# A two-layer token kernel: who masks the first energies of the second attention's later steps, when GpSimd masks the others, and where the gelu table is loaded

## The chip, the cores and the metric

The kernel runs on one core of one Trainium2 chip. The metric is device time in microseconds (us) of one execution. The engines are called TensorE (PE), VectorE (DVE), ScalarE (ACT), GpSimd (POOL) and SyncE (SP) here; PE's weight loads are a lane of their own (PEld) in the profile.

## What is computed

Input: 8192 tokens (32 x 256) of 128 features, all fp32. Two layers, each of the form x = x + attention(norm(x)) + mixture_of_experts(norm(x)). Layer 0 has a linear attention and a gated expert layer with a shared expert. Layer 1, in which the change lies, is:

```python
q = elu(x @ Wq.T + bq); k = elu(x @ Wk.T + bk)          # 8 heads of 16
v = silu(x @ Wv.T + bv); u = silu(x @ Wu.T + bu)
mask = tril(ones(256, 256))
energy = einsum('bhnd,bhmd->bhnm', q, k) * mask          # no softmax
out = einsum('bhnm,bhmd->bhnd', energy, v)
x_att = (u * rms_norm(out, scale)) @ Wo.T + bo

probs = softmax(x @ w_router.T); top 2 of 8 experts per token
h = gelu(x @ w1[e] + b1[e])                              # 128 -> 512
out = sum over the two experts of gate * (h @ w2[e] + b2[e])
```

Only the blocks of 128 x 128 on the diagonal of the mask need a mask; the off-diagonal half comes from a running state.

## The kernel before, in words

The tokens are 16 groups of 512 (`NG` = 16). The program is written out by hand for each engine; each engine runs its list in order, and semaphores tie them together. Its parts in time are the first attention with the shared expert (to about 150 us), the 36 expert tiles of layer 0 (to about 410 us), the second attention (to about 640 us), and the 36 expert tiles of layer 1 to the end.

**The second attention** is a software pipeline of steps 2 to 17. In step s, group g = s - 2 gets its q, k, v and u, group e = s - 3 its energies and their product with v, and groups y = s - 4 and x = s - 5 their norm and their addition to x. A group's energies come in two sets, i = 2e and i = 2e + 1. Each set fills two pairs of PSUM banks of 128 x 1024: `pair[2]` and `pair[3]`.

- PE computes a set (L1101). `energies(e, 1)` may overwrite the banks only when both halves of `energies(e, 0)` are read.
- DVE multiplies `pair[2]` by the causal mask on the way to SBUF (L1718, `mask_energies`).
- ACT copies `pair[3]` to SBUF unmasked (L2095, `copy_energies`), and POOL masks that copy in place (L2321, `affine_select`). For the last two groups (e >= `DVE_MASKS` = 14) DVE masks the copy in place (L1724).
- PE multiplies the masked sets by v (`gather`, L1124).

**What else DVE does in a step.** In order: q's elu (L1690), adding a finished group to x (L1743), `mask_energies(e, 0)`, k's elu (L1690), routing arithmetic and `shift` (L1282), v (L1699), `mask_energies(e, 1)`, u (L1706), the state (L1710), and `gated` (L1731). In steps 3, 4 and 6 to 10 it also joins layer 0's expert results to x (`collect0`, L1655), eight instructions of 128x128 with both inputs in SBUF. Step 10 does the last join (group 15). Routing arithmetic (L1288 to L1408) is small instructions of 128x128 or less, most with both inputs in SBUF.

**What POOL does in a step.** Eight indirect transfers, numbered 0 to 7 (gathers of expert results, L2215, or sends of routed rows, L2204); between them two masks, and a power for the root (L2326, or L2331 `powers`, which DVE's next L1736 waits for). Each of the first transfers waits for a semaphore of PE's step (`behind_attention1`). The order before is: transfers 0, 1, mask of set 2e, 2, 3, mask of set 2e + 1, root, 4, 5, 6, `powers`, 7.

Of the kernel before, what the change touches and what calls it, by code (L numbers as in the profile page):

```python
# [12 lines left out]
ACT = mybir.ActivationFunctionType  # L13
AX = mybir.AxisListType.X

P = 128
# [4 lines left out]
NG = NT // GT  # L21
# [88 lines left out]
LEAD = 2  # L110
# [2 lines left out]
STEPS0 = NG + LEAD + 2  # L113
STEPS1 = NG + LEAD + 3
DVE_MASKS = NG - 2


NSTAGE, NIN, NOUT, NJOIN, NGATE, AHEAD = (8, 4), 4, 4, 3, 2, 6
# [41 lines left out]
def with_root(y):  # L160

    return STATS[1].get(y + LEAD + 2, (None,))[0]
# [7 lines left out]
def masked_by_dve(e):  # L170

    return e >= DVE_MASKS


def columns_before(layer, step):
# [77 lines left out]
def build(nc, t, out):  # L253
    const_np, at = constants()
    with ExitStack() as ctx:
        pe, dve, act, pool, sp = nc.tensor, nc.vector, nc.scalar, nc.gpsimd, nc.sync
# [74 lines left out]
        def const(name):  # L331
            a, n = at[name]
            return consts[:, a:a + n]

        ident = const("ident")
# [172 lines left out]
        def blocks(ap, b=P):  # L508
            return ap.rearrange("p (a b) -> p a b", b=b)
# [165 lines left out]
        def tensor_program():  # L675
# [409 lines left out]
            def energies(e, s):  # L1085

                i = 2 * e + s
                if i == 0:
                    pe.wait_ge(ranks_read, NS + 1)
                    pe.wait_ge(out_ready, NTILES)  # L1090
                    pe.wait_ge(hid_ready, 2 * NTILES)
                if i >= 1:
                    pe.wait_ge(en_dve, i)
                    pe.wait_ge(en_copied, i)
                pe.wait_ge(q1_ready, e + 1)
                pe.wait_ge(kh1_ready, e + 1)
                for tile in range(GT):
                    tok = slice(tile * P, (tile + 1) * P)
                    for r in range(ROWTILES):
                        part = slice(32 * r, 32 * r + 32)  # L1100
                        m = pe.matmul(bank[4 + r][:, tok], kh1[e % 2][s][part, tok], q1[e % 2][part, tok], start=True, stop=True)  # L1101
                m.then_inc(en_done, 1)
# [14 lines left out]
            def gather(e, s):  # L1117
                i = 2 * e + s
                pe.wait_ge(en_dve, i + 1)
                pe.wait_ge(en_masked, i + 1)  # L1120
                for tile in range(GT):
                    for j in range(ROWTILES):
                        c = ((j % 2) * GT + tile) * P
                        m = pe.matmul(bank[3][32 * j:32 * j + 32, tile * P:(tile + 1) * P],  # L1124
                                      v_heads[e % 2][:, tile, j, s:s + 2, :].rearrange("p s d -> p (s d)"), en1[j // 2][i % 2][:, c:c + P],
                                      start=False, stop=(s == HEADS32 - 1 and tile == GT - 1), skip_group_check=True)
                m.then_inc(av_done, 1)
# [122 lines left out]
        def vector_program():  # L1250
# [462 lines left out]
            def mask_energies(e, s):  # L1713
                i = 2 * e + s
                dve.wait_ge(en_done, i + 1)
                if i >= 2:
                    dve.wait_ge(av_done, i - 1)
                dve.tensor_tensor(blocks(en1[0][i % 2][:]), blocks(pair[2][:]),  # L1718
                                  const("causal").unsqueeze(1).to_broadcast([P, 8, P]), ALU.mult).then_inc(en_dve, 1)

            def mask_copied(e, s):
                i = 2 * e + s
                dve.wait_ge(en_copied, i + 1)
                dve.tensor_tensor(blocks(en1[1][i % 2][:]), blocks(en1[1][i % 2][:]),  # L1724
                                  const("causal").unsqueeze(1).to_broadcast([P, 8, P]), ALU.mult).then_inc(en_masked, 1)

# [102 lines left out]
        def scalar_program():  # L1829
# [267 lines left out]
            def squares(e):  # L2097
                act.wait_ge(uo_ready, e + 1)
                if e >= 1:
                    act.wait_ge(ss_done, e)  # L2100
                act.activation(sq1[:], bank[3], ACT.Square).then_inc(sq_ready, 1)
# [7 lines left out]
            for step in range(LEAD, NG + LEAD):  # L2109
                g, e, y = step - LEAD, step - LEAD - 1, step - LEAD - 2  # L2110
                new, old, last = 0 <= g < NG, 0 <= e < NG, 0 <= y < NG
                if new and g >= 1:
                    minus_exp(q1_done, g, 0, e1[0], q1_max, q1_exp)
                    minus_exp(k1_done, g, 1, e1[1], k1_max, k1_exp)
                if last:
                    squares(y)
                if old:
                    copy_energies(e, 0)
                if new:
                    tanh1(v1_done, g, 0, th1[0], v1_ready, v1_tanh)  # L2120
                if has_sums(1, step):
                    keep_sums(1, step, 0 if last else P, P * (1 + len(LOGITS[1].get(step, ()))))
                if new:
                    queries1(g)
                if old:
                    copy_energies(e, 1)
                if last:
                    totals(y)
                if step in LOGITS[1]:
                    keep_logits(1, step)  # L2130
                if new:
                    tanh1(u1_done, g, 1, th1[1], u1_ready, u1_tanh)
                    if step == LEAD:
                        columns(1, EX_LATER[0], 6)
                    keys_by_token(g)
                for n in COLUMNS[1].get(step, ()):
                    if n not in EX_LATER:
                        normalise(1, n)

                two = len(COLUMNS[1].get(step, ())) > 1  # L2140
                if new and not two:
                    heads1(g)
                for k, n in enumerate(COLUMNS[1].get(step, ())):
                    columns(1, n, 1 - k)
                if new and two:
                    heads1(g)
                for _, s, names in ROUTE[1].get(step, ()):
                    if "b" in names:
                        exponentials(1, s)

            squares(NG - 2)
            copy_energies(NG - 1, 0)
            copy_energies(NG - 1, 1)
# [34 lines left out]
        def pool_program():  # L2188
# [128 lines left out]

            def mask_energies(e, s):
                i = 2 * e + s
                pool.wait_ge(en_copied, i + 1)  # L2320
                pool.affine_select(out=blocks(en1[1][i % 2][:]), in_=blocks(en1[1][i % 2][:]), pattern=[[0, 8], [1, P]], compare_op=ALU.is_ge,  # L2321
                                   fill=0.0, base=0, channel_multiplier=-1).then_inc(en_masked, 1)

# [9 lines left out]
            for step in range(LEAD, NG + LEAD + 1):  # L2333
# [12 lines left out]
                            send(1, *sends[i - len(gathers)])  # L2346

                transfer(0)
                transfer(1)
                if old and not masked_by_dve(e):  # L2350
                    mask_energies(e, 0)
                transfer(2)
                transfer(3)
                if old and not masked_by_dve(e):
                    mask_energies(e, 1)
                if last and with_root(y) is None:
                    roots(y)
                transfer(4)
# [76 lines left out]
```

## Time and profile before

| | |
|---|---|
| median of 3 runs | 897.45 us (894.57 to 899.02) |
| the profiled execution | 900.08 us, of which the span is 898.5 us |
| PE busy | 92% of the span |
| DVE busy | 78% |
| POOL busy | 69% |
| ACT busy | 65% |
| second attention, 421.0 to 627.0 us | 206 us for steps 3 to 17, 12.5 to 15 us each |

Times are from the start of the span. The profile is of one execution, so what is worked out of it is compared with 900.08 us, not with the median. Within a step of the second attention the shares differ much from those of the whole: DVE is busy for 10.8 to 14.2 us of each step.

### The profile page before, as it was taken

What the parts mean: (1) busy time and instruction counts of PE and PEld (TensorE: products, weight loads), DVE (VectorE), ACT (ScalarE), POOL (GpSimd) and SP (SyncE); (2) the same over time, 40 slices, a digit from 0 to 9 for tenths busy, and PEclk for the clock granted to TensorE, in tenths of its full rate; (3) what the DMA queues carried; (4) which work ended last, traced back from release to release, by engine and by line L of the source; (5) the groups of instructions that cost most, each with busy time, mean ns of one, the idle gap of its engine ahead of it and who ended that gap; (6) DMA issues with size and microseconds to landing.
All of it is one profiled execution on the core that took longest, in us unless ns stands there. A gap on an engine that the chain in (4) does not pass through costs nothing.

```text
span 898.5 us, 22649 instructions
## 1 busy us (share of the span) xinstructions
PE 827.5 (92%) x7937; PEld 737.8 (82%) x7937; DVE 700.3 (78%) x1812; ACT 581.1 (65%) x1190; POOL 623.8 (69%) x599
## 2 busy tenths in 40 slices
PE   5789989999899989998898889898999999999996
PEld 3678878889799989986665666566899999999995
DVE  6787788987577987897889998999765566567776
ACT  5756465545366667768887777665776666666660
POOL 4157777777005788785888888888877777777662
PEclk9999999999999989999999999999999999999998
DMA  9799998116659997972111111113766555678976
GB/s 264 236 372 357 357 353 296 53 54 192 216 165 274 319 304 225 288 226 78 42 42 37 37 41 42 44 42 121 288 186 213 176 173 186 198 236 268 290 248 206
DMA packets 130995, 173.98 MB, mean 194 GB/s; under 512 B 15810, under 2 KB 85954, under 8 KB 130628
## 3 DMA queue, kind: packets, MB, share of 16 engines
q1 hardware_dynamic: 96864, 124.43, 42.6%
q0 software_dynamic: 16640, 34.37, 11.9%
q10 hardware_dynamic: 17380, 13.73, 5.1%
q8 instruction: 65, 1.06, 0.5%
q14 instruction: 46, 0.38, 0.1%
HBM read 93.64 MB, written 80.97 MB: 194 GB/s over the span
## 4 chain that ended last, share of the span: by engine, by line
PE 48%; DVE 26%; issue 7%; POOL 6%; ACT 5%; SPq 5%; DMA 3%; DVEq 0%; ACTq 0%; POOLq 0%
PE pair L977 14%; PE pair L913 5%; PE pair L915 5%; PE pair L914 5%; POOL sent L2204 4%; PE pair L944 3%; PE pair L822 3%; DVE a_en L1718 2%; PE pair L733 2%; DVE X L1655 2%; DVE stats_t L1266 2%; SPq L618 2%; ACT a_rows L1845 2%; SPq L590 1%; PE pair L1101 1%
## 5 line engine op out<-in xcount | busy, mean ns | idle before, releaser
L2204 POOL DMA_INDIRECT sent<-a_rows,slot x224 | 224.0, 1000 | 68.1 <-issue 64.5
L2215 POOL DMA_INDIRECT ex_joined<-outs,slot x128 | 135.5, 1059 | 88.9 <-DMA outs<-ex_tile_out 50.5
L913 PE MATMUL pair<-ex_x_hi,ex_w_hi 128*128 128x256 f32 x497 | 146.5, 295 | 0.2 <-issue 0.2
L915 PE MATMUL pair<-ex_x_hi,ex_w_lo 128*128 128x256 f32 x497 | 140.4, 282 | 0.0
L914 PE MATMUL pair<-ex_x_lo,ex_w_hi 128*128 128x256 f32 x497 | 140.3, 282 | 0.0
L2306 POOL DMA_INDIRECT back<-ex_tile_out,slot x104 | 113.9, 1096 | 36.8 <-issue 26.5
L977 PE MATMUL pair<-ex_down_all,ex_hid 128*128 x1136 | 133.3, 276 | 0.5 <-issue 0.3
L977 PEld LDWEIGHTS pair<-ex_down_all,ex_hid 128*128 128x128 f32 x1136 | 129.7, 192 | 2.3 <-issue 2.3
L2019 ACT ACTIVATE ex_hid<-pair,ex_stage 128x256 f32<-128x256 f32 x284 | 107.5, 491 | 6.8 <-PE pair L915 3.4
L1881 ACT ACTIVATE ex_w_hi<-ex_stage 128x768 fp32r<-128x768 f32 (+1 forms) x72 | 67.4, 937 | 52.4 <-DMA ex_stage<-in_experts 52.4
L913 PEld LDWEIGHTS pair<-ex_x_hi,ex_w_hi 128*128 128x128 f32 x497 | 94.8, 191 | 0.6 <-issue 0.6
L914 PEld LDWEIGHTS pair<-ex_x_lo,ex_w_hi 128*128 128x128 f32 x497 | 94.7, 191 | 0.0
L915 PEld LDWEIGHTS pair<-ex_x_hi,ex_w_lo 128*128 128x128 f32 x497 | 94.6, 190 | 0.0
L1483 DVE TENSOR_TENSOR ex_w_lo<-ex_stage,ex_w_hi 128x768 fp32r<-128x768 f32 (+1 forms) x72 | 77.2, 1072 | 6.2 <-ACT ex_w_hi L1881 5.8
L944 PE MATMUL pair<-ex_stage,ex_hid 128*128 128x128 f32 x568 | 71.3, 280 | 0.9 <-DVE ex_hid L1611 0.9
L1627 DVE TENSOR_TENSOR ex_tile_out<-pair,ex_b2o 128x512 f32<-128x512 f32 (+1 forms) x31 | 20.6, 666 | 64.5 <-PE pair L977 64.5
L944 PEld LDWEIGHTS pair<-ex_stage,ex_hid 128*128 128x128 f32 x568 | 68.2, 196 | 2.1 <-issue 1.7
L2009 ACT ACTIVATE ex_gate_s<-pair 128x512 f32<-128x512 f32 (+1 forms) x72 | 42.2, 587 | 32.0 <-PE pair L915 27.3
L1489 DVE TENSOR_TENSOR ex_x_lo<-pair,ex_x_hi 128x512 fp32r<-128x512 f32 x72 | 48.9, 680 | 14.9 <-ACT ex_x_hi L1887 14.4
L1611 DVE TENSOR_TENSOR ex_hid<-ex_gate_s,pair 128x512 f32<-128x512 f32 (+1 forms) x72 | 48.9, 680 | 9.7 <-ACT ex_gate_s L2009 6.5
L1845 ACT ACTIVATE a_rows<-X,shift,rstd 128x128 f32<-128x128 f32 x88 | 36.2, 485 | 30.8 <-DVE shift L1282 30.8
L1887 ACT ACTIVATE ex_x_hi<-pair 128x512 fp32r<-128x512 f32 x72 | 42.4, 588 | 20.1 <-PE pair L733 20.0
(269 smaller groups left out, 2025.7 us busy)
## 6 DMA issues: line engine op xcount, KB each, us to landing
outs<-v_heads SPq DMA_DIRECT2D x8, 4352.0 KB, 37.7
ex_stage<-in_experts SPq DMA_DIRECT2D x72, 322.0 KB, 3.5
ex_stage<-in_experts SPq DMA_DIRECT2D x72, 320.0 KB, 5.0
ex_tile_in<-sent SPq DMA_DIRECT2D x72, 128.0 KB
outs<-ex_tile_out SPq DMA_DIRECT2D x71, 128.0 KB
ex_joined<-back ACTq DMA_DIRECT2D x15, 512.0 KB, 5.8
ex_tile_in<-sent SPq DMA_DIRECT2D x54, 132.0 KB
X<-in_x SPq DMA_DIRECT2D x16, 256.0 KB, 5.0
```

Of the source, the lines that this page charges most:

```text
L913: pe.matmul(o[:, of_half], wh, x_hi[i % 2][:, of_half], start=True, stop=False)
L914: pe.matmul(o[:, of_half], wh, x_lo[i % 2][:, of_half], start=False, stop=False)
L915: m = pe.matmul(o[:, of_half], wl, x_hi[i % 2][:, of_half], start=False, stop=True)
L944: m = pe.matmul(bank[7][:, i * C:(i + 1) * C], hid[n % 2][c][:, i * P:(i + 1) * P], stage[0][n % NSTAGE[0]][:, i // HALF, 2 * F0P + c * C: ...
L977: m = pe.matmul(bank[b][:, s * C:(s + 1) * C], hid[n % 2][c][:, s * P:(s + 1) * P], down_all[:, bass.ds(experts[s // HALF], 1), c * C:(c + ...
L1483: dve.tensor_tensor(w_lo[layer][n % NSTAGE[layer]][:, 0:k, 0:u], stage[layer][n % NSTAGE[layer]][:, 0:k, 0:u], w_hi[i % 2][:, 0:k, 0:u].bi ...
L1845: m = act.activation(r[:, (g % GPS) * GT + j, 0:C], X[:, n, :], ACT.Identity, bias=shift[:, n:n + 1], scale=inverse_of(layer, g)[:, j:j + 1])
L1881: act.activation(w_hi[i % 2][:, 0:k, 0:u], stage[layer][n % NSTAGE[layer]][:, 0:k, 0:u], ACT.Copy).then_inc(w_hi_here, 1)
L2019: m = act.activation(hid[n % 2][c][:, of_half], bank[bank_of_up1(n, c)][:, of_half], ACT.Gelu, bias=stage[1][n % NSTAGE[1]][:, h, b1:b1 + 1])
L2204: pool.indirect_dma_start(out=sent[layer], out_offset=bass.IndirectOffsetOnAxis(ap=slot_i[layer][k][:, s, j:j + 1], axis=0), in_=rows[laye ...
L2215: pool.indirect_dma_start(out=joined[g % NJOIN][:, j, k, :], out_offset=None, in_=outs, in_offset=bass.IndirectOffsetOnAxis(ap=slot_i[0][k ...
L2306: pool.indirect_dma_start(out=back, out_offset=bass.IndirectOffsetOnAxis(ap=address_of(n)[:, s // HALF, s % HALF:s % HALF + 1], axis=0), i ...
```

## The change

Three edits.

1. **First masks of late steps.** For even sets i = 2e with 8 <= e < 14 (steps 11 to 16, behind the last join) DVE masks `pair[3]` too, straight from PSUM, right behind `pair[2]`. ACT's copy and POOL's mask of these six sets are gone. `en_dve` is signalled behind the second of the two.
2. **POOL's masks.** Where POOL still masks, the mask of set 2e stands behind transfer 0 instead of 1, and that of set 2e + 1 behind transfer 2 instead of 3 (steps 3 to 16).
3. **Gelu.** Behind its last step and ahead of `squares(14)`, ACT runs a gelu of 1x8 on constants.

```diff
+FROM_PSUM = max(s for s in STATS[1] if STATS[1][s] == (NG - 1,)) - LEAD      # 8
+def masked_from_psum(i):
+    return i % 2 == 0 and FROM_PSUM <= i // 2 < DVE_MASKS
+def copies_before(i):
+    return sum(not masked_from_psum(j) for j in range(i))
...
 # tensor_program, energies(e, s)
                 if i >= 1:
                     pe.wait_ge(en_dve, i)
-                    pe.wait_ge(en_copied, i)
+                    pe.wait_ge(en_copied, copies_before(i))
...
 # tensor_program, gather(e, s)
-                pe.wait_ge(en_masked, i + 1)
+                pe.wait_ge(en_masked, copies_before(i + 1))
...
 # vector_program, mask_energies(e, s)
-                dve.tensor_tensor(blocks(en1[0][i % 2][:]), blocks(pair[2][:]),
-                                  const("causal").unsqueeze(1).to_broadcast([P, 8, P]), ALU.mult).then_inc(en_dve, 1)
+                m = dve.tensor_tensor(blocks(en1[0][i % 2][:]), blocks(pair[2][:]), const("causal").unsqueeze(1).to_broadcast([P, 8, P]), ALU.mult)
+                if masked_from_psum(i):
+                    m = dve.tensor_tensor(blocks(en1[1][i % 2][:]), blocks(pair[3][:]), const("causal").unsqueeze(1).to_broadcast([P, 8, P]), ALU.mult)
+                m.then_inc(en_dve, 1)
...
 # scalar_program, a step
-                if old:
+                if old and not masked_from_psum(2 * e):
                     copy_energies(e, 0)
...
+            act.wait_ge(q1_max, NG)
+            act.activation(e1[0][0:1, 0:8], ident[0:1, 0:8], ACT.Gelu)
             squares(NG - 2)
...
 # pool_program, a step
                 transfer(0)
+                if old and not masked_by_dve(e) and not masked_from_psum(2 * e):
+                    mask_energies(e, 0)
                 transfer(1)
-                if old and not masked_by_dve(e):
-                    mask_energies(e, 0)
                 transfer(2)
-                transfer(3)
                 if old and not masked_by_dve(e):
                     mask_energies(e, 1)
+                transfer(3)
```

POOL's queue from the end of step 9 through step 10, before. `powers` is step 9's; `sent` and `ex_joined` rows are transfers; `a_en_111` is the copy of set 2e, `a_en_112` that of set 2e + 1.

```order
L2331 TENSOR_TENSOR powers<-bases,halves_of 128x8
L2215 DMA ex_joined_144<-outs,slot 128x128
L2204 DMA sent<-ex_rows_147,slot 69632x132 x2
L2321 AFFINE_SELECT a_en_111<-a_en_111 128x1024
L2204 DMA sent<-ex_rows_147,slot 69632x132 x2
L2321 AFFINE_SELECT a_en_112<-a_en_112 128x1024
L2204 DMA sent<-ex_rows_147,slot 69632x132 x3
```

The same place in the changed kernel.

```order
L2346 TENSOR_TENSOR powers<-bases,halves_of 128x8
L2230 DMA ex_joined_144<-outs,slot 128x128
L2219 DMA sent<-ex_rows_147,slot 69632x132
L2336 AFFINE_SELECT a_en_111<-a_en_111 128x1024
L2219 DMA sent<-ex_rows_147,slot 69632x132 x2
L2336 AFFINE_SELECT a_en_112<-a_en_112 128x1024
L2219 DMA sent<-ex_rows_147,slot 69632x132 x4
```

Both masks stand one transfer sooner; the number of instructions is the same.

POOL's queue in step 11, before.

```order
L2204 DMA sent<-a_rows_85,slot 69632x132 x2
L2321 AFFINE_SELECT a_en_111<-a_en_111 128x1024
L2204 DMA sent<-a_rows_85,slot 69632x132 x2
L2321 AFFINE_SELECT a_en_112<-a_en_112 128x1024
L2326 TENSOR_TENSOR rms<-rms,halves_of 128x4
```

The same place in the changed kernel.

```order
L2219 DMA sent<-a_rows_85,slot 69632x132 x3
L2336 AFFINE_SELECT a_en_112<-a_en_112 128x1024
L2219 DMA sent<-a_rows_85,slot 69632x132
L2341 TENSOR_TENSOR rms<-rms,halves_of 128x4
```

The mask of set 2e is gone, and the other has three transfers ahead of it instead of four and a mask.

DVE's queue in step 13, before: from the addition to x to v. `a_en_109` is the masked `pair[2]` of set 2e, and the small instructions on `gatev` and `cells` are routing.

```order
L1743 SCALAR_TENSOR_TENSOR X<-pair,rms,X 128x128 x4
L1718 TENSOR_TENSOR a_en_109<-pair,consts 128x1024
L1690 SCALAR_TENSOR_TENSOR a_k<-pair,bqk1p,a_e_94 128x512
L1339 TENSOR_REDUCE gatev<-route 128x16
L1340 TENSOR_TENSOR cells<-route 128x128
L1341 TENSOR_REDUCE gatev<-cells 128x16
```

The same place in the changed kernel.

```order
L1756 SCALAR_TENSOR_TENSOR X<-pair,rms,X 128x128 x4
L1729 TENSOR_TENSOR a_en_109<-pair,consts 128x1024
L1731 TENSOR_TENSOR a_en_111<-pair,consts 128x1024
L1701 SCALAR_TENSOR_TENSOR a_k<-pair,bqk1p,a_e_94 128x512
L1350 TENSOR_REDUCE gatev<-route 128x16
L1351 TENSOR_TENSOR cells<-route 128x128
```

A second instruction of 128x1024 stands ahead of k's elu; all behind it keeps its order.

## Rows read from the trace of the kernel before

**Rows 1.** Chain that ended last, 412 to 500 us; columns: start, us, what.

```profile
by line: POOL sent L2204 20.1%; issue 11.9%; DVE X L1655 8.7%; DVE a_en L1718 5.7%; POOL a_en L2321 5.0%; POOL ex_joined L2215 4.4%; POOL powers L2331 3.9%; PE pair L1101 3.8%; DVE X L1743 3.1%; DVE a_u L1706 2.9%; POOL rstd L2198 2.4%; DVE
...
476.17 1.69 POOL powers L2331
```

**Rows 2.** Chain that ended last, 626 us to the end, by line.

```profile
by line: PE pair L977 46.7%; PE pair L913 12.6%; PE pair L915 12.4%; PE pair L914 12.4%; PE pair L733 5.7%; DMA ex_joined<-back 2.2%; PE pair L1101 1.0%; PE pair L1124 0.8%; DVE X L1666 0.8%; issue 0.8%; DVE X L1665 0.7%; DVE a_en L1718 0.5
```

**Rows 3.** DVE in order of time, steps 7 and 8: start, us, instruction, idle before.

```profile
479.35 1.22 DVE L1718 TENSOR_TENSOR a_en<-pair,consts 128x1024 f32<-128x1024 f32 x1
...
481.13 1.56 DVE L1282 SCALAR_TENSOR_TENSOR shift<-moments,powers 128x4 f32<-128x4 f32 x1
...
484.42 0.67 DVE L1706 SCALAR_TENSOR_TENSOR a_u<-a_th,pair 128x512 f32<-128x512 f32 x1
485.01 2.23 DVE L1655 SCALAR_TENSOR_TENSOR X<-ex_joined,gates_tok,X 128x128 f32<-128x128 f32 x4
...
487.49 1.25 DVE L1655 SCALAR_TENSOR_TENSOR X<-ex_joined,gates_tok,X 128x128 f32<-128x128 f32 x4
...
494.74 1.22 DVE L1718 TENSOR_TENSOR a_en<-pair,consts 128x1024 f32<-128x1024 f32 x1
...
499.31 0.69 DVE L1706 SCALAR_TENSOR_TENSOR a_u<-a_th,pair 128x512 f32<-128x512 f32 x1 [0.57 <-ACT a_th L2082]
```

**Rows 4.** Busy time of line L1655 in steps 7 to 10: us, DVE busy.

```profile
478.00:534.90 56.90, 12.52 (x32) 1.00 0.13 39
```

**Rows 5.** POOL in order of time, step 7.

```profile
485.07 1.10 POOL L2321 TENSOR_SCALAR_AFFINE_SELECT a_en<-a_en 128x1024 f32<-128x1024 f32 x1
...
490.42 1.66 POOL L2331 TENSOR_TENSOR powers<-bases,halves_of 128x8 f32<-128x8 f32 x1 [0.42 <-DVE bases L1273]
```

**Rows 6.** DVE in order of time, steps 11, 13, 15 and 16.

```profile
539.13 1.25 DVE L1289 TENSOR_TENSOR cells<-logit,gatev 128x128 f32<-128x128 f32 x1
540.42 0.32 DVE L1290 TENSOR_TENSOR cells<-cells,consts 128x128 f32<-128x128 f32 x1
...
565.50 1.54 DVE L1340 TENSOR_TENSOR cells<-route 128x128 f32<-128x128 f32 x1
...
592.68 0.99 DVE L1330 CAST slot<-gatev 128x16 int32<-128x16 f32 x1
593.71 0.17 DVE L1331 CAST slot<-gatev 128x16 int32<-128x16 f32 x1
...
596.65 0.58 DVE L1363 CAST starts_i<-ends 128x8 int32<-128x8 f32 x1
...
605.58 1.67 DVE L1388 TENSOR_TENSOR cells<-tiles_f,cells 128x136 f32<-128x136 f32 x1
```

**Rows 7.** DVE in order of time, step 13, a mask and what follows.

```profile
563.40 1.22 DVE L1718 TENSOR_TENSOR a_en<-pair,consts 128x1024 f32<-128x1024 f32 x1
564.53 0.74 DVE L1690 SCALAR_TENSOR_TENSOR a_k<-pair,bqk1p,a_e 128x512 f32<-128x512 f32 x1
```

**Rows 8.** PE in order of time, steps 11, 14 and 18.

```profile
543.72 0.66 PE L680 MATMUL pair<-consts,a_rows 128*128 128x128 f32 x4 [0.38 <-DVE a_u L1706]
...
578.46 0.22 PE L711 MATMUL pair<-choice_bf,before_bf 128*128 128x128 bf16 x1 [0.88 <-DVE choice_bf L1305]
...
579.50 1.17 PE L1101 MATMUL pair<-a_q,a_kh 32*128 32x128 f32 x32 [0.77 <-DVE a_en L1718]
...
628.58 1.70 PE L1101 MATMUL pair<-a_q,a_kh 32*128 32x128 f32 x32 [1.71 <-DVE a_en L1718]
```

**Rows 9.** Two stretches: us, busy PE, PEld, DVE, ACT, POOL, granted PE clock, DMA.

```profile
577.50:580.70 3.20, 1.55 (x40) 1.21 (x36) 3.10 (x8) 1.30 (x4) 2.70 (x4) 1.00 0.13 42
629.00:632.40 3.40, 3.40 (x52) 2.54 (x48) 3.40 (x4) 2.08 (x3) 2.79 (x3) 0.51 0.95 382
```

**Rows 10.** Start of layer 1's expert tiles, ACT and PE in order of time.

```profile
639.64 1.28 ACT L2019 ACT_TABLE_LOAD   x1
...
641.92 0.36 PE L913 MATMUL pair<-ex_x_hi,ex_w_hi 128*128 128x256 f32 x1 [0.17 <-issue]
```

More of the change, by code:

```diff
@@ L1717, in mask_energies @@
                     dve.wait_ge(av_done, i - 1)
-                dve.tensor_tensor(blocks(en1[0][i % 2][:]), blocks(pair[2][:]),
-                                  const("causal").unsqueeze(1).to_broadcast([P, 8, P]), ALU.mult).then_inc(en_dve, 1)
+                m = dve.tensor_tensor(blocks(en1[0][i % 2][:]), blocks(pair[2][:]), const("causal").unsqueeze(1).to_broadcast([P, 8, P]), ALU.mult)
+                if masked_from_psum(i):
+                    m = dve.tensor_tensor(blocks(en1[1][i % 2][:]), blocks(pair[3][:]), const("causal").unsqueeze(1).to_broadcast([P, 8, P]), ALU.mult)
+                m.then_inc(en_dve, 1)
             def mask_copied(e, s):
                 i = 2 * e + s
-                dve.wait_ge(en_copied, i + 1)
+                dve.wait_ge(en_copied, copies_before(i + 1))
                 dve.tensor_tensor(blocks(en1[1][i % 2][:]), blocks(en1[1][i % 2][:]),
@@ L2319, in mask_energies @@
                 i = 2 * e + s
-                pool.wait_ge(en_copied, i + 1)
+                pool.wait_ge(en_copied, copies_before(i + 1))
                 pool.affine_select(out=blocks(en1[1][i % 2][:]), in_=blocks(en1[1][i % 2][:]), pattern=[[0, 8], [1, P]], compare_op=ALU.is_ge,
```

## The prediction

> **What bounds the kernel now.** I read the chain that ended last first, cut at the stretches of the change. From 626 us to the end it is PE almost alone: four matmul lines hold 84% [rows 2]. The reader is to see that nothing behind the second attention can swallow or add time: whatever the second attention gains is handed on one to one. In the second attention up to 500 us the chain runs over POOL's transfers (L2204 20%, L2215 4%), POOL's masks (5%) and `powers` (4%), and over DVE [rows 1]. It still passes `powers` at 476.17, the one that DVE waits for at the start of step 7 [rows 1]. So to step 6 POOL is the bound, and its list gets no shorter there; from step 7 on DVE is, with PE a little behind it.
>
> Next I read DVE instruction by instruction, and looked for rows much longer than their own kind. They are the core of this case. The addition of a join takes 1.25 us for four (487.49), but 2.23 at 485.01 [rows 3], and POOL's mask runs from 485.07 to 486.17 [rows 5]. `shift` takes 1.56 us for 4 columns [rows 3]. In steps 11, 13, 15 and 16 one small routing instruction each takes 1.25, 1.54, 0.99 and 1.67 us, where its like takes 0.32 or 0.17 [rows 6]. Each of them lies under a mask of POOL. So POOL's mask costs DVE time when DVE meets it with an instruction whose inputs are in SBUF, and costs none under L1718, L1690 or L1706, which read PSUM.
>
> **Edit 2, masks one transfer sooner, steps 3 to 10.** Nothing is added. A mask moves ahead by about 1.3 us (a transfer of 0.97 and the 0.30 in front of it) against DVE's work. The second mask then lies under L1718 and u instead of under the joins. In steps 7 to 10 L1655 holds DVE for 12.52 us in 32 instructions [rows 4]; eight quartets of 1.25 [rows 3] would be 10.0, so 2.5 us are waits. Of the 0.98 in step 7 I leave 0.2, because everything ahead of the join also starts sooner there: gain 2.3 us. The first mask stood over `shift`. What this is worth is less than the stall itself, since u has a floor: from the mask at 494.74 to u at 499.31 are 4.57 us although DVE stood idle for 0.57 of them, waiting for PE and ACT [rows 3]. Step 7 took 5.07 (479.35 to 484.42) [rows 3]: gain 0.5. In steps 8 to 10 the floor is already met: gain 0. In steps 3 to 6 DVE loses several us to masks as well, but POOL's own list sets the time. It could run `powers` of step 6 only some 0.3 us sooner: gain 0.3, with 0 and 1.8 as ends. Behind step 7 POOL has little slack itself (0.42 idle ahead of `powers` [rows 5]), and takes back 0.2 by step 10. Sum of edit 2: -2.9 us, with ends 0 and -4.5.
>
> **Edit 1, six first masks by DVE.** Added: six instructions like L1718. One holds DVE for 1.13 us (563.40 to 564.53) [rows 7]: 6.8 us in all. Removed: six copies on ACT, which isn't waited for there, and six masks on POOL, whose worth is what DVE waits for under them [rows 6]. By steps, in us:
>
> - 13, 15, 16, where DVE itself is the chain: 1.13 - (1.54 - 0.29) = -0.1; 1.13 - (0.99 - 0.17) = +0.3; 1.13 - (1.67 - 0.30) = -0.2.
> - 11: DVE alone would lose 1.13 - 0.93 = 0.2. But PE's `energies(e, 1)` waits for `en_dve`, which comes 1.13 later, and PE's list behind it must reach L680, where it now waits 0.38 for u [rows 8]. So PE is late by 0.75: +0.7.
> - 14: PE stood 0.77 for the mask at 579.50 [rows 8], and no mask of POOL is in DVE's way: +1.1, all of it on the chain.
> - 12: PE has no wait and DVE some: between 0 and 1.13, +0.6.
>
> The set 2e + 1 is masked by POOL sooner too, as a mask and a transfer ahead of it are gone. The earliest is when ACT has copied it, and DVE is by then at v and L1718, which read PSUM. It also leaves the cast at 596.65 (0.58 instead of 0.17) [rows 6]: -0.4. Sum of edit 1: +2.4 - 0.4 = +2.0 us, with ends 0 and +6.8.
>
> One price isn't in DVE's list. PE stood 1.71 us ahead of 628.58 [rows 8], and right behind that wait the granted clock was 0.51 over 629.0 to 632.4 (the lower of the two levels, 1.2 GHz) [rows 9]. In step 14 PE stood 0.88 and 0.77 with two short matmuls between, and the clock stayed 1.00 [rows 8, 9]. The second wait now becomes 0.77 + 1.13 = 1.90, so that of some 3 us hardly 0.3 are work. That is more idleness than what was punished at 628. I take one fall there. Half clock for 3.4 us would lose at most 1.7; some of it falls on waits, so +1.3, with ends 0 and 1.7.
>
> **Edit 3, gelu's table.** The load of 1.28 us stands at 639.64 on ACT, in front of the first gelu. PE lacks only 0.17 us there (641.92), as it has matmuls of the next tile ahead [rows 10]. The new place is in a wait of ACT for u's product. Gain 0.2, ends 0 and 0.5.
>
> **Sum.** -2.9 + 2.0 + 1.3 - 0.2 = +0.2 us on the profiled 900.08, which lies 2.6 above the median of 897.45. Moved to the median: 897.6, which I round to 897.5.
>
> **A rule weighed.** DVE's L1388 began at 605.58, and undisturbed would have ended at 605.88; POOL's mask is recorded from some 0.1 us after that. It took 1.67 all the same [rows 6]. The Trainium skill (SBUF — State Buffer, Who interferes with whom) says that the pair of ports shared by DVE and GpSimd is an exclusive lock for a whole instruction, and that the order of issue decides who waits. By that order DVE should have won here and at 565.50, and the long rows would have another cause that the change leaves in place.
>
> **Rivals.**
>
> - **A cause other than the mask (0.05).** If the waits at 565.50 and 605.58 aren't the mask's, 1.25 + 1.37 = 2.6 us of edit 1's return is missing: +2.8, 900.3 us. Against it: no such row is found in steps 12 and 14, where the first mask met PSUM instructions. The lock's order of issue, named above, is what speaks for it.
> - **The masks only change their victims (0.13).** The moved masks meet other SBUF instructions, since DVE too starts sooner. Edit 2 then gives 0.5 instead of 2.9: +2.6, 900.0 us. It decides where the second mask still overlaps L1655 by 1 us in steps 8 to 10.
> - **The clock falls in each step with a lengthened wait (0.12), slower.** In steps 11, 13, 14 and 16 `energies(e, 1)` waits up to 1.13 us longer for DVE. If PE falls to 1.2 GHz in all four, three more falls at 1.3 come on top: +0.2 + 3.9 = +4.1, 901.6 us, and with the ends of edit 1 a little over 902. It decides where waits of 1.5 us suffice; at 628.58 it took 1.71 [rows 8].
> - **The joins were worth more, and the added masks are hidden (0.15), faster.** If POOL follows DVE in steps 5 and 6, 1.5 more come back, and if PE and DVE have slack in steps 11 to 16, edit 1 costs nothing and no clock falls: -2.9 - 1.5 - 0.2 = -4.6, 892.9 us. POOL's chain up to 476 speaks against the first half [rows 1], the 0.77 in step 14 against the second.
>
> **How the numbers follow.** My case, gains and losses that cancel, gets 0.55; its own range is 895 to 900.5, which holds the sum without a fall of the clock (-1.1) too. The range 892.5 to 902 reaches to the fast and the slow rival. About 0.5%, or 4.5 us, is what a measurement of this kernel can tell from no change. Only the fast rival and the tails cross it below (0.17), only the clock rival's upper half and tails above (0.10); the rest, 0.73, is no change.
>
> **What would show it.** In the changed profile: L1655 in steps 7 to 10 busy for about 10.2 us instead of 12.5. Routing instructions in steps 11, 13, 15 and 16 all near 0.3. DVE's two masks back to back, 1.13 apart, and PE waiting for the second ahead of `energies(e, 1)`, 1.9 in step 14. A granted clock under 1 in step 14. ACT's table load before 627 us. POOL idle in steps 12 to 16 where it never was. The first add of the expert phase's chain begins within 1.5 us of where it began. The prediction is wrong if DVE meets masks of POOL in places that I took as free, or if a wait for `powers` or a root appears on DVE.

## The result, and the profile after

The changed kernel took 901.33 us (median of 20 runs, 897.34 to 904.55), the kernel before 898.86 us (20 runs on the same chip, 894.57 to 900.73). The ratio is 1.0029, 95% interval 1.0015 to 1.0042: slower by some 2.6 us (1.3 to 3.8). That lies inside the forecast range of 892.5 to 902 us, and within the 0.5% that the forecast called no change. The forecast was a balance of +0.2 us. The gains and losses that it named are there, but some of their sizes are off, and the profile and the experiments show which.

The profiled execution of the changed kernel took 901.92 us, of which the span is 900.5. The first part of its page:

```profile
span 900.5 us, 22638 instructions
## 1 busy us (share of the span) xinstructions
PE 828.0 (92%) x7937; PEld 738.5 (82%) x7937; DVE 695.0 (77%) x1818; ACT 576.4 (64%) x1185; POOL 618.4 (69%) x593
```

The shares say nothing here: six instructions more on DVE, six fewer on POOL and six copies fewer on ACT. What tells is the length of each step. I take it as the time from a step's first mask on DVE (L1718 before, L1729 after) to the next step's. In the table, rows e1 to e12 are the experiments of the next section. The lengths are worked out from the rows of that line, with the granted clock of step 14 beside them, in all profiled executions on chips where the kernel before runs in 897 to 899 us:

| us | 3-6 | 7-10 | 11 | 12 | 13 | 14 | 15 | 16 | clock in 14 |
|---|---|---|---|---|---|---|---|---|---|
| before | 57.39 | 57.68 | 12.53 | 13.84 | 14.83 | 11.37 | 13.87 | 12.70 | 1.00 |
| after | 57.76 | 55.17 | 13.42 | 14.08 | 16.88 | 14.04 | 14.34 | 13.06 | 0.88 |
| e1, edit 2 | 57.81 | 55.15 | 12.29 | 13.53 | 16.03 | 14.00 | 13.38 | 11.99 | 0.76 |
| e2, edit 1 | 57.41 | 57.68 | 13.42 | 14.11 | 15.35 | 14.05 | 14.12 | 12.90 | 0.88 |
| e3, edit 3 | 57.42 | 57.72 | 12.53 | 13.85 | 14.82 | 12.91 | 14.16 | 11.97 | 0.87 |
| e4, short masks | 57.75 | 55.17 | 12.50 | 13.45 | 14.39 | 11.58 | 13.20 | 12.12 | 1.00 |
| e9, chosen steps | 57.40 | 55.18 | 12.29 | 13.50 | 14.29 | 12.90 | 13.38 | 11.97 | 0.87 |
| e10, copied | 57.42 | 57.70 | 14.13 | 13.85 | 15.26 | 13.10 | 15.37 | 13.28 | 0.87 |
| e11, copied, late | 57.41 | 57.71 | 13.77 | 14.84 | 16.10 | 14.16 | 14.76 | 15.79 | 0.88 |
| e12, split signal | 57.40 | 57.67 | 13.41 | 14.09 | 15.30 | 15.14 | 14.09 | 12.87 | 0.78 |

Steps 3 to 13 repeat to some 0.03 us where nothing touches them, and that is what makes this table worth more than ten totals. Steps 15 and 16 repeat only where step 14 had the same clock. In e3, which changes nothing in them, they took 14.16 and 11.97 us behind a slower step 14, against 13.87 and 12.70 before: POOL's masks met other instructions of DVE (1.55 us at L1326 and 0.74 at L1387, instead of 0.99 at L1330 and 1.67 at L1388). The table also sets right two ranges given for the kernel before: its steps 3 to 17 took 10.8 (step 17) to 15.4 us, and DVE was busy for only 9.5 us of step 14.

The totals aren't that steady. Step 3's first mask started anywhere from 418.0 to 423.8 us in these executions, though no code ahead of it differs. After against before, steps 3 to 16 took 4.54 us more, the changed kernel entered them 3.95 us sooner by chance, and took 1.4 more behind them: the 2.0 us between the two spans.

**Edit 2 in the profile after.** Line, engine, shape, count, busy us and mean ns, over steps 7 to 10:

```profile
L1666 DVE SCALAR_TENSOR_TENSOR X<-ex_joined,gates_tok,X 128x128 f32<-128x128 f32 x32 | 10.0, 355 | 0.3
```

10.0 us instead of 12.52 [rows 4]; no join meets a mask there any more. But DVE now waits longer for POOL's `powers` ahead of step 7 (0.61 us before) and also ahead of step 11 (no such wait before), and the gain of step 6 isn't there. DVE in order of time, with the idle time before in brackets:

```profile
474.31 0.17 DVE L1749 TENSOR_SCALAR rms<-powers 128x4 f32<-128x4 f32 x1 [1.40 <-POOL powers L2346]
...
529.48 0.17 DVE L1749 TENSOR_SCALAR rms<-powers 128x4 f32<-128x4 f32 x1 [0.56 <-POOL powers L2346]
```

**Edit 1 in the profile after.** DVE in step 13, where 565.50 had taken 1.54 us [rows 6]:

```profile
558.44 1.21 DVE L1729 TENSOR_TENSOR a_en<-pair,consts 128x1024 f32<-128x1024 f32 x1
559.58 1.21 DVE L1731 TENSOR_TENSOR a_en<-pair,consts 128x1024 f32<-128x1024 f32 x1
...
561.67 0.29 DVE L1351 TENSOR_TENSOR cells<-route 128x128 f32<-128x128 f32 x1
...
565.14 0.69 DVE L1717 SCALAR_TENSOR_TENSOR a_u<-a_th,pair 128x512 f32<-128x512 f32 x1 [0.43 <-ACT a_th L2095]
567.38 0.42 DVE L1721 TENSOR_TENSOR a_kv<-pair,consts 128x256 f32<-128x256 f32 x1 [1.55 <-PE pair L1092]
```

The masks stand 1.14 apart and the routing instruction takes 0.29, as forecast. New are the two waits at the end. PE in steps 13 and 14 shows where they come from:

```profile
560.84 1.17 PE L1112 MATMUL pair<-a_q,a_kh 32*128 32x128 f32 x32 [1.54 <-DVE a_en L1731]
...
562.56 1.91 PE L1080 MATMUL pair<-xT,w_attn 128*128 128x512 f32 x2
...
577.72 1.17 PE L1112 MATMUL pair<-a_q,a_kh 32*128 32x128 f32 x32 [1.90 <-DVE a_en L1731]
...
579.29 1.91 PE L1080 MATMUL pair<-xT,w_attn 128*128 128x512 f32 x2
```

The wait of 1.90 is the forecast one (0.77 before [rows 8]). L1080 took 1.91 us in both steps and takes 1.02 at full clock. The granted clock of the two places (us, then busy PE, PEld, DVE, ACT, POOL, the clock, DMA):

```profile
562.00:566.00 4.00, 4.00 (x28) 2.61 (x30) 3.29 (x7) 2.58 (x6) 2.63 (x3) 0.57 0.01 3
577.50:583.50 6.00, 5.78 (x75) 4.00 (x75) 3.80 (x8) 3.35 (x6) 3.11 (x3) 0.72 0.04 14
```

So there were two falls toward the lower level (1.2 GHz) in this execution, in steps 13 and 14, where I had forecast one. Step 13 of e2 has the same wait of 1.54 us and stayed at 1.00.

**Edit 3 in the profile after.** The table is loaded early, and ACT's first expert weights come no sooner:

```profile
623.51 1.28 ACT L2165 ACT_TABLE_LOAD   x1
...
639.64 1.06 ACT L1894 ACTIVATE ex_w_hi<-ex_stage 128x1024 fp32r<-128x1024 f32 x1 [0.94 <-DMA ex_stage<-in_experts]
```

### The profile page after: what moved, and what is told of

It reads as the page before. It is cut to its first block, busy times and chain, and to the rows that moved or that the text cites. A ratio compares the mean times of both kernels' runs of the same rounds, so it can differ in the third digit from the quotient of the medians.

```text
span 900.5 us, 22638 instructions
## 1 busy us (share of the span) xinstructions
PE 828.0 (92%) x7937; PEld 738.5 (82%) x7937; DVE 695.0 (77%) x1818; ACT 576.4 (64%) x1185; POOL 618.4 (69%) x593
## 4 chain that ended last, share of the span: by engine, by line
PE 51%; DVE 22%; ACT 6%; issue 6%; POOL 6%; DMA 5%; SPq 4%; DVEq 0%; POOLq 0%; ACTq 0%
PE pair L988 14%; PE pair L926 5%; PE pair L924 5%; PE pair L925 5%; PE pair L955 3%; POOL sent L2219 3%; PE pair L833 3%; PE pair L744 2%; ACT a_rows L1858 2%; DVE X L1666 2%; DVE stats_t L1277 2%; PE pair L1112 2%; POOL ex_joined L2230 2%; SPq L629 1%; PE pair L1080 1%
```

## The experiments

Ratios are to the kernel before on the same chip, run alongside; in brackets are 95% intervals. e1 to e4 ran against a kernel before of 897.70 us.

**e1_order, e2_masks, e3_gelu: one edit at a time.** Their diffs are the three parts of the change: POOL's order alone, `masked_from_psum` with all that hangs on it alone, the two lines of gelu alone.

> The kernel before with edit 2 alone: POOL's masks one transfer sooner in steps 3 to 16. My theory: edit 2 gains 2.9 us, most of it in steps 7 to 10, and edit 1 is what costs more than I gave it. Then this one is at 0.9968 of before, and the instructions of the join in steps 7 to 10 take about 10.4 us in all. Rival A, the masks only change their victims, or POOL, now the bound in steps 5 to 7 and 10, takes the gain back: 0.9995 to 1.0005. In the changed kernel steps 7 to 10 together were 2.5 us shorter (57.68 to 55.17) but the start of the second attention also lay 3.7 us earlier for no reason that the change gives; if that is the reordering too (rival B), this one is at 0.993.

> The kernel before with edit 1 alone: six first sets masked by DVE from PSUM, POOL's other masks where they were. By the step lengths of the changed kernel (steps 11 to 16 took 6.7 us longer: 0.9, 0.2, 2.1, 2.7, 0.5, 0.4) my theory expects 1.0065 to 1.0075 of before, and the clock below 1 in steps 13 and 14. As I predicted it, the edit and its clock fall cost 3.3 us: 1.0037. Rival: if the step lengths owe their growth to the masks of POOL that stand one transfer sooner in these steps (its second mask waits 1.2 to 4.4 us for the copy of ACT), this one is below 1.003.

> The kernel before with edit 3 alone: the small gelu ahead of squares(14). Predicted: 0.2 us gained, 0.9998. Rival: in the changed kernel the expert phase lost 1.2 us at its start, where the table had been loaded already and a transfer of expert weights landed 1.7 us later than before; if that comes with the edit, 1.001 to 1.002, and the wait of ACT for the staged weights is seen at about 639 us again.

Measured: e1 0.9964 (0.9941 to 0.9987), e2 1.0039 (1.0017 to 1.0062), e3 1.0005 (0.9985 to 1.0026). In us: -3.2, +3.5, +0.4, each to about 2 us. So the total of edit 2 agrees with what I had said (-2.9), that of edit 1 with its clock too (+3.3), and edit 3 can't be told from nothing, nor from my -0.2, nor from most of its rival's 1.001 to 1.002. The three add up to +0.7, less than the 2.6 of the whole change, but within their intervals. Rival B of e1 is ruled out: its second attention began at 423.2 us, so the early start in the changed kernel wasn't the reordering. Two sharper expectations failed. e2 was to be at 1.0065 or more, with the clock below 1 in steps 13 and 14; that size was read off one execution with two falls, and e2's step 13 was at 1.00. The joins of e1 took 10.0 us instead of 10.4.

e1 shows a victim that I hadn't foreseen. DVE at the end of step 13, and POOL there:

```profile
575.81 0.36 DVE L1304 TENSOR_TENSOR route<-cells,gatev 128x128 f32<-128x128 f32 x1
576.21 1.88 DVE L1305 TENSOR_TENSOR choice_bf<-route 128x128 bf16<-128x128 f32 x1
```

```profile
576.82 1.11 POOL L2321 TENSOR_SCALAR_AFFINE_SELECT a_en<-a_en 128x1024 f32<-128x1024 f32 x1
```

Step 14's first mask, one transfer sooner, now meets step 13's last routing instruction, right ahead of the mask that PE waits for. It costs 1.6 us there. PE then stood 2.54 us for `choice_bf`, and the granted clock of step 14 was 0.76, the lowest of the table. In the changed kernel that mask doesn't exist (edit 1 took it away), which is why it isn't seen there.

**e4_short: what edit 1 costs is the instruction.**

```diff
-                    m = dve.tensor_tensor(blocks(en1[1][i % 2][:]), blocks(pair[3][:]), const("causal")...to_broadcast([P, 8, P]), ALU.mult)
+                    m = dve.tensor_tensor(en1[1][i % 2][:, 0:P], pair[3][:, 0:P], const("causal"), ALU.mult)
```

> The changed kernel, but the second mask of DVE covers 128x128 instead of 128x1024 (seven eighths of these six sets stay unmasked and uncopied, so that part of the energies is left out). It takes 1.0 us off DVE and off the release of the banks in each of six steps and leaves everything else. My theory, that the price of edit 1 is the 1.13 us per step that DVE and behind it PE stand in line, and the falls of the clock that follow from the longer waits: 0.9970 of before, no clock below 1 in steps 13 and 14, steps 11 to 16 as long as before or shorter. Rival, that it comes from elsewhere (POOL's mask waiting for the copy with its transfers behind it, the wait for the second copy): 1.001 or more, steps 11 to 16 still 3 us or more longer.

Here the second mask covers an eighth of its width; seven eighths of these sets are left unmasked and uncopied, so the kernel leaves out part of the energies. Measured: 0.9932 (0.9908 to 0.9955). Against the changed kernel that is 0.0097, or 8.7 us, for six times 1.0 us of DVE. Steps 11 to 16 took 77.24 us instead of 85.82, and step 14 ran at full clock:

```profile
572.60:584.10 11.50, 10.34 (x157) 7.34 (x158) 9.65 (x25) 6.22 (x12) 7.67 (x9) 1.00 0.10 35
```

In the four steps where neither kernel had a fall, 1.0 us less of DVE gave 0.92, 0.63, 1.14 and 0.94 us. So the six masks are on the path almost one for one, and the rest of the 8.6 us, 2.6, goes with the two clock falls. Steps 11 to 16 took 1.9 us less than before here. That isn't what the removed masks and copies of edit 1 bring, as edit 2 stands in it: e9 below, where POOL's masks are only moved, took 0.8 us less than before in the same steps with a fall of 1.5 us among them.

**e5_chosen, e6_copied, e7_one14, e8_split: on another chip.** That chip ran the kernel before in 1034.25 us. In the four profiles from there, DVE stood again and again in the second attention for releasers that the trace calls remote: 0.5 to 3.4 us at a time in steps 4 to 16, and 3.0 to 9.4 us in step 17. The kernel before wasn't profiled there. e5 leaves POOL's order as before in steps 3 to 6 and 14. e6 has ACT copy the six sets as before and DVE mask the copies. e7 has edit 1 in step 14 alone. e8 signals DVE's two masks one by one:

```diff
 # e5: sooner = step in (7, 8, 9, 10, 11, 12, 13, 15, 16)
+                if not sooner:
+                    transfer(1)
                 mask_energies(e, 0)
+                if sooner:
+                    transfer(1)                   # and transfer(3) likewise around the other
 # e6
+def dve_in_place(e, s):
+    return masked_by_dve(e) or s == 0 and 8 <= e < DVE_MASKS
 # e7, masked_from_psum
+    return i == 2 * 11
 # e8, energies(e, s), where set i - 1 is masked from PSUM
+                for half in ((0, 1), (2, 3)):      # bank[4 + r] for r in half
+                    if half[0] == 2:
+                        pe.wait_ge(en_dve, masks_before(i))
```

> The kernel before with edit 2 only in steps 7 to 13, 15 and 16: steps 3 to 6 and step 14 keep POOL's order. With edit 2 everywhere, steps 3 to 6 together became 0.4 us longer, steps 7 to 10 2.5 shorter, 11, 12, 15 and 16 0.2 to 0.7 shorter each, and step 13 1.2 us longer, because step 14's first mask, one transfer sooner, met the last routing instruction of step 13 (1.88 us). My theory: with step 14 left alone that stall is gone, step 13 is 0.7 shorter than before, and the sum is -4.2 us: 0.9953. Rival, that the stall of step 13 only moves on, since POOL's list is as long as before: step 13 or 14 at least 1 us longer than in the kernel before, 0.997 or more.

> The kernel before, but the six first sets are copied by ACT as before and masked in place by DVE right behind its first mask, instead of by POOL. DVE has the same 1.13 us more per step as with edit 1, but the banks are released by ACT's copy, so PE need not wait for DVE's second mask ahead of energies(e, 1). With edit 1 alone steps 11 to 16 took 0.9, 0.3, 0.5, 2.7, 0.25 and 0.2 us more than before, and DVE then waited 0.69, 1.08, 0.51, 1.72, 0, 0.43 us for PE ahead of the state. My theory, that the excess over my prediction is this late release: steps 11 and 13 at +0.2 and +0.0, step 14 no more than +1.1 without a clock fall; 1.001 to 1.0025. Rival, that DVE's 1.13 us is the whole price wherever the banks come free: the same step lengths as with edit 1 alone, 1.004 to 1.0055.

> The kernel before with edit 1 in step 14 alone. My theory: step 14 is 1.13 us longer by the mask, and 1.5 us more where the granted clock falls in it; the fall comes with or without the mask (step 14 had it in an execution with the gelu edit alone, 12.91 us, and not in that of before, 11.37). So 12.5 or 14.0 us for step 14, the others as before, 1.0013 as ratio. Rival, that the mask brings the fall, as I predicted: step 14 at 14.0 us, 1.003, and a mean granted clock below that of before by 0.002.

> The kernel before with edit 1 alone, but DVE signals each of its two masks by itself, and PE writes the first pair of banks of energies(e, 1) behind the first and the second pair behind the second (the matmuls are the same, their order over the banks is not). If the late release is what edit 1 costs beyond DVE's own list, PE's wait of 1.5 us ahead of energies(e, 1) is cut by about the half set it can do in it, 0.5 us, and steps 11, 13 and 16 shrink by 0.3 to 0.5 each against edit 1 alone: 1.0025. Rival, that DVE's time alone counts: no change from edit 1 alone, 1.004 or more.

Measured: e5 1.0096 (1.0060 to 1.0132), e6 1.0013 (0.9987 to 1.0039), e7 1.0012 (0.9984 to 1.0040), e8 1.0047 (1.0024 to 1.0069). e5 is slower there, against my expectation and against e9 below. DVE in its step 9:

```profile
567.68 1.23 DVE L1718 TENSOR_TENSOR a_en<-pair,consts 128x1024 f32<-128x1024 f32 x1 [1.89 <-remote]
```

Its steps 8 to 10 took 15.8, 16.7 and 15.3 us, where e6 and e7 on the same chip took 14.0 to 14.3. Why the sooner masks lose there stays open. e7's step 14 took 16.04 us and its ratio is as expected, but with steps 11 to 13 up to 3 us longer than on the other chips I don't count it as evidence. By the same measure e6, whose 1.0013 is what my theory asked for, and e8, whose 1.0047 is what its rival asked for, decide nothing. Three of the four ideas were tried again or in another form.

**e9_chosen_again, e10_copied_again** ran against 899.10 us.

> The kernel of e5_chosen again (edit 2 in steps 7 to 13, 15 and 16 alone). The chip of e5 to e8 ran the kernel before in 1034 us and put stops in PE's and DVE's way whose releaser the trace doesn't name; nothing under 1% can be read there. My theory is the same: steps 7 to 10 2.5 us shorter, 11 and 12 0.2 to 0.3 shorter each, step 13 0.7 shorter since step 14's mask stays out of its routing, 0.9953. Rival, that the sooner masks cost what they bring wherever they stand: 0.999 or more.

> The kernel of e6_copied again (ACT copies the six first sets, DVE masks the copies in place). On the other chip DVE no longer waited for PE ahead of the state in step 11 (0.19 or more in the others there), but other stops covered the sum. My theory, that the late release of the banks is what edit 1 costs beyond DVE's own list: steps 11 to 16 0.0 to 0.2 us longer than before in 11, 13, 15 and 16, +0.3 in 12, +1.1 in 14: 1.0015 without and 1.003 with a fall of the clock in 14. Rival, that DVE's 1.13 us is the whole price: the step lengths of edit 1 alone (+0.9, +0.3, +0.5, +1.1 and 1.5 for the clock, +0.25, +0.2), 1.004.

Measured: e9 0.9966 (0.9951 to 0.9982), e10 1.0039 (1.0019 to 1.0059). e9's steps 7 to 13 are as expected (step 13 0.54 shorter instead of 0.7), and the stall of 1.88 is gone. The forecast 0.9953 lies within the interval. In the profiled execution step 14 took 12.90 us, 1.5 more than before. That step is word for word the one of before, and so it is in e3. Here are PE's rows in e3, whose waits are those of [rows 8] to the hundredth:

```profile
575.05 0.22 PE L711 MATMUL pair<-choice_bf,before_bf 128*128 128x128 bf16 x1 [0.88 <-DVE choice_bf L1305]
...
576.09 1.46 PE L1101 MATMUL pair<-a_q,a_kh 32*128 32x128 f32 x32 [0.77 <-DVE a_en L1718]
...
578.18 1.91 PE L1069 MATMUL pair<-xT,w_attn 128*128 128x512 f32 x2
```

The clock fell here without any mask of edit 1. The fall is worth 12.91 - 11.37 = 1.5 us in its step (1.1 by the end of step 16, since steps 15 and 16 of e3 were 0.4 shorter), and the fallen step 14 of e2 (14.05) lies 1.14 above this one.

e10's total speaks for the rival, its rows for my theory with a new loss on top. PE had its banks after 0.44 us (1.57 in e2), first e2 then e10:

```profile
535.98 1.17 PE L1112 MATMUL pair<-a_q,a_kh 32*128 32x128 f32 x32 [1.57 <-DVE a_en L1731]
```

```profile
534.65 1.17 PE L1106 MATMUL pair<-a_q,a_kh 32*128 32x128 f32 x32 [0.44 <-DVE a_en L1723]
```

With it, in these steps, the wait of DVE ahead of the state went, which in e2 was 0.69, 0.51 and 0.43 us in steps 11, 13 and 16. Step 14 took 13.10, only 0.19 more than e3's with the same clock. But POOL's remaining mask, a mask sooner than before, met `shift`. e10, DVE and POOL:

```profile
537.62 1.62 DVE L1287 SCALAR_TENSOR_TENSOR shift<-moments,powers 128x4 f32<-128x4 f32 x1
```

```profile
538.11 1.11 POOL L2326 TENSOR_SCALAR_AFFINE_SELECT a_en<-a_en 128x1024 f32<-128x1024 f32 x1
```

Likewise 1.40 us in step 15 and 1.12 in step 16. In step 13 it met a small instruction:

```profile
565.54 0.72 DVE L1348 TENSOR_TENSOR gatev<-gatev 128x16 f32<-128x16 f32 x1
```

With these stalls counted, e10's steps follow DVE's own list. Each is the added 1.13, less the stall that went, plus the new one: in step 11, 1.13 - 0.96 + 1.46 = 1.63 us (measured 1.60), in step 13, 1.13 - 1.25 + 0.55 = 0.43 (0.43), in step 16, 1.13 - 1.37 + 0.84 = 0.60 (0.58).

**e11_copied_late, e12_split_again** ran against 897.10 us. e11 is e10 with `transfer(4)` ahead of POOL's remaining mask in steps 11 to 16.

> As e10_copied_again (ACT copies the six first sets, DVE masks the copies in place), but in steps 11 to 16 POOL's remaining mask stands one transfer later, where it stood before. In e10 the wait of DVE for PE ahead of the state was gone in steps 11, 13 and 16 (0.69, 0.51, 0.43 us with edit 1 alone), and step 14 cost 0.2 us against an execution with the same clock; but POOL's mask, 1.3 us sooner since the first was gone, met shift (1.62 us), a cast (1.40) and past (1.12), and steps 11, 15 and 16 became 1.6, 1.5 and 0.6 us longer. My theory, that these are the mask's victims again: with the mask 1.27 us later it lies under v, the second mask and u, which read PSUM; steps 11 and 15 at most 0.4 us longer than before, 0.9995 to 1.0015. Rival, that DVE's own added 1.13 us is the price: 1.004 again.

> The kernel of e8_split again (edit 1 alone, each of DVE's two masks signalled by itself, PE filling the first pair of banks in between) on a chip without the stops of the other. Edit 1 alone had steps 11 to 16 at 13.42, 14.11, 15.35, 14.05 (with a fall of the clock), 14.12 and 12.90 us, and DVE waited 0.69, 0.51 and 0.43 us for PE ahead of the state in steps 11, 13 and 16. If the late release of the banks is what that edit costs beyond DVE's list, half a set done in the wait takes 0.4 to 0.5 us off 11, 13, 14 and 16: 1.002. Rival: the step lengths of edit 1 alone, 1.004.

Measured: e11 1.0092 (1.0061 to 1.0122), e12 1.0043 (1.0022 to 1.0064). Both expectations failed. In e11's step 11 `shift` took 0.16 us again, so the mask had been its cause. But the transfer put ahead had to wait for PE, and the mask came 1.6 us later than meant and met the next instruction from SBUF. POOL, then DVE:

```profile
542.60 0.96 POOL L2209 DMA_INDIRECT sent<-a_rows,slot  x1 [1.72 <-PE pair L1129]
543.57 1.11 POOL L2326 TENSOR_SCALAR_AFFINE_SELECT a_en<-a_en 128x1024 f32<-128x1024 f32 x1
```

```profile
543.31 1.52 DVE L1300 TENSOR_TENSOR route<-cells,a_rows 128x128 f32<-128x128 f32 x1
```

Its long step 16 (15.79 us) had a second cause, a fall of the clock there too: 0.78 over the step, behind a wait of PE of only 0.32 us.

In e12 PE began as early as hoped, and gained nothing:

```profile
540.18 2.29 PE L1121 MATMUL pair<-a_q,a_kh 32*128 32x128 f32 x32 [0.44 <-DVE a_en L1738]
```

The 32 matmuls took 2.29 us instead of 1.17, and ended where they end in e2: 0.44 + 2.29 = 2.73, 1.57 + 1.17 = 2.74. Steps 11, 12, 13, 15 and 16 are within 0.05 us of e2's; step 14 was 1.1 us longer, at a clock of 0.78 instead of 0.88. The start of the set, e2 and then e12, busy time of this line's matmuls and their count:

```profile
535.90:536.50 0.60, 0.52 (x16) 1.00 0.33 113
```

```profile
540.10:540.70 0.60, 0.52 (x8) 1.00 0.33 113
```

Over two banks PE did 8 matmuls in the time of 16 over four, so half a set takes as long as a whole one, and the early start is used up.

## Why the prediction was right, and where not

The time came out inside the range since large gains and losses cancelled, as the prediction said. The balance was 2.4 us off, and that it wasn't more is in part luck: the terms of both edits were too favourable, and the 1.3 us charged for a fall of the clock covered some of that without being shown to be the edit's.

**What bounds (right).** What is won or lost in the steps isn't taken back behind them. Behind step 17's first mask the kernels took 282.3 to 285.2 us, with no relation to the steps: before 282.33, e4 282.44, after 283.74. But this spread of 2.9 us is as large as the effect, so a single total shows little.

**Edit 2 (mechanism right, its sum partly by luck).** Steps 7 to 10 gave 2.51 us where the terms 2.3, 0.5 and -0.2 said 2.6; L1666 is at 10.0 against a forecast 10.2. Steps 3 to 6 gave nothing where I took 0.3: they became 0.4 longer. The waits of DVE for `powers` became longer there (in e1 1.51 us instead of 0.90 and 1.03 instead of 0.61); why POOL's list came later isn't shown. So steps 3 to 10, which my -2.9 was for, gave -2.1. e1's -3.2 has steps 11 to 16 in it, for which edit 2 alone had no term, and an interval of 2 us on either side; its closeness to -2.9 is luck. The rival "masks only change their victims" is refuted for steps 7 to 10. It is true in step 13 of e1, and in step 4, where `shift` went from 0.15 to 1.76 us in e1 as a join went from 2.73 to 2.12.

**Edit 1 (mis-sized).** Without any clock, e2 against before (and in step 14 against e3) gives +0.89, +0.27, +0.52, +1.14, +0.25 and +0.20 for steps 11 to 16: 3.3 us, where the record has +2.0. Against e3 in steps 15 and 16 too, where the clock of step 14 is about the same, it is -0.04 and +0.93, and 3.7 in all. Steps 11 and 14 were close (0.7 and 1.1), step 12 smaller than I had (0.6). The failed step is "13, 15, 16, where DVE itself is the chain": there the removed stall was to pay for the new mask. In 13 and 16 DVE then stood 0.51 and 0.43 us for PE ahead of the state. PE's list from the release of the banks to the state is nearly as long as DVE's, and in edit 1 both begin behind the second mask, so a removed stall pays only until DVE reaches PE: in step 13 1.25 - 0.51 = 0.74 us of it. I had worked out PE's lateness for step 11 and not carried it to its neighbours. Two other runs bear this out. e4's second mask is 1.0 us shorter and DVE's waits are the same (0.70, 0.50 and 0.43 us in steps 11, 13 and 16); e1 has none of the added masks, and where its stall is gone, in step 11, DVE waits as long. First e4 in step 13, then e1 in step 11:

```profile
564.60 0.42 DVE L1721 TENSOR_TENSOR a_kv<-pair,consts 128x256 f32<-128x256 f32 x1 [0.50 <-PE pair L1092]
```

```profile
542.52 0.42 DVE L1710 TENSOR_TENSOR a_kv<-pair,consts 128x256 f32<-128x256 f32 x1 [0.71 <-PE pair L1081]
```

e10 shows the other side: with the banks released by ACT's copy, ahead of the added mask, these waits are gone, the steps follow DVE's list, and step 14 costs 0.2 instead of 1.1.

**The clock (size about right, cause not borne out).** I gave one fall in step 14 to the wait of 1.90. The fall is real (0.88, and 0.72 over the 6 us at it), and worth 1.5 us in its step. But e3 and e9 have it in an unchanged step 14 behind waits of 0.88 and 0.77, while the execution of before with the same waits, and e4 with 0.87 and 0.97, were spared. I took the one execution of before for the rule, so the term of 1.3 charged to the edit what the unchanged kernel also pays in some executions. Whether edit 1 brings more falls on average isn't shown. The mean granted clock of a run is 0.9890 in the changed kernel (20 runs) and 0.9914 in the kernel before (68 runs on three chips). e2 and e12, with edit 1, are both 0.0020 below the kernel before on their chips. But e3, which changes nothing in these steps, is 0.0011 below too, and e9 and e10 are 0.0021 and 0.0027 above. Among the runs of before a difference of 0.001 goes with 0.6 to 0.9 us; 0.0024 would be 1.4 to 2.2 us, an estimate from these runs, if the difference is real. Of the rival that the clock falls in 11, 13, 14 and 16, steps 11 and 16 are refuted: waits of 1.57 and 1.54 us left them at 1.00 in the changed kernel. Step 13 did fall there, behind 1.54 us, and not in e2, behind the same wait.

**Signs named ahead.** Seen: L1666 near 10.2, routing instructions near 0.3, masks 1.13 apart with 1.90 in step 14, a clock under 1 there, the table load ahead of 627 us, and POOL idle in steps 12 to 16 (its remaining mask waited 4.38 us for ACT's copy in step 14). One was missed, if the first sum of joined expert rows is taken for it: it began at 802.8 us (L1665) before and 1.9 us later (804.7) in the changed kernel, not within 1.5. Among the signs of a wrong prediction, longer waits for `powers` were there (1.40 and 0.56 us), and so were masks in places that I had taken as free (`choice_bf` in e1).

**Edit 3 (not settled).** The load was hidden, as said. Of 0.2 us nothing can be told at this precision. At the first gelu, ACT stood 0.94 for staged weights in the changed kernel; e1, without edit 3, had 0.49 there, and e3, with it, 0.19, so this wait isn't the edit's.

**The sum.** By steps, after against before without the clock: +0.4 - 2.5 + 3.3 = +1.2. The measured 2.6 leaves 1.4 over; more falls of the clock would give about that (1.4 to 2.2), but this isn't settled, and the interval of the measured time begins at 1.3. The record had -2.9 + 2.0 + 1.3 - 0.2. The rival that the long rows have another cause than the mask is refuted: with the masks gone, 565.50's successor takes 0.29 and that of 605.58 0.30, and e10 and e11 each bring a stall back where a mask of POOL is put. The fast rival, that the added masks are hidden, is refuted by e2's six longer steps.

**The better kernel** is edit 2 alone: 0.9964 in all steps, 0.9966 in chosen ones. On the slower chip the latter lost 1%, so it isn't a safe gain.

## What to carry to other kernels

Where a stall is removed and work put in its place, follow the added work to every other engine that waits for its signal; the stall's owner is not the only one who pays. A mask of POOL can't be judged by where it stands in its own list, only by which instruction of DVE it then meets: moved by one transfer it freed 2.5 us in four steps and took 1.6 in one. And compare a pipeline by its step lengths, which here repeated to 0.03 us up to the first fall of the clock, while totals moved by several us.

## What the runs showed of the hardware that I had not expected

- By the records, DVE is held before POOL's mask begins. In e10 `shift`, which took 0.16 us in e11, began at 537.62 and ended with the mask (538.11 + 1.11 = 539.22), 0.49 us ahead of it; in e1 `choice_bf` began 0.61 us ahead (576.21 and 576.82) and took 1.88 us, 0.29 in step 13 of before. Undisturbed, both would have ended ahead of the mask. The Trainium skill (SBUF — State Buffer, Who interferes with whom) would give the shared ports to the first to issue, for its whole instruction; these rows don't agree, if POOL's recorded start is its real one.
- One and the same step, with the same waits in front (0.88 and 0.77 us), ran at a granted clock of 1.00 in one execution (before) and 0.87 in two others (e3, e9).
- Matmuls of 32 rows ran at half the rate when they went over two banks and groups of 32 rows at a time instead of four (e12 and e2: 8 instead of 16 in 0.52 us, all 32 in 2.29 instead of 1.17).
